# Softmax sums of a fourth attention layer split between GpSimd and VectorE, and a bias moved from GpSimd to ScalarE

## What is computed

```python
qt = conv1x1(x, w_q, b_q).reshape(BS * N_HEADS, H * W, -1)
xp = avg_pool_3x3_s2_same(x)
kt = conv1x1(xp, w_k, b_k).reshape(BS * N_HEADS, H * W // 4, -1)
vt = conv1x1(xp, w_v, b_v).reshape(BS * N_HEADS, H * W // 4, -1)
attn = jnp.einsum('bnd,bmd->bnm', qt, kt) / TEMP
attn = jax.nn.softmax(attn, axis=-1)
out = jnp.einsum('bnm,bmd->bnd', attn, vt)
out = conv1x1(out.reshape(BS, H, W, -1), w_o, b_o)
return out + x
```

## Time and profile before

| what | us |
|---|---|
| median of 3 runs | 139.18 |
| lowest, highest | 138.91, 140.83 |
| the profiled execution | 138.04 |
| its span, first to last instruction | 136.2 |
| busy in it: PE, DVE, ACT, POOL | 121.5, 91.3, 76.1, 59.7 |

### The profile page before, as it was taken

The page is one execution under the profiler, slowest core; times in us unless marked ns, Lnnn a source line. Parts: engine busy times, 40 slices in busy tenths (PEclk is TensorE's granted clock), DMA queues, the critical chain, the costliest instruction groups (busy, mean ns, idle before and its releaser), DMA issues.

```text
span 136.2 us, 3586 instructions
## 1 busy us (share of the span) xinstructions
PE 121.5 (89%) x1391; PEld 90.1 (66%) x1391; DVE 91.3 (67%) x212; ACT 76.1 (56%) x226; POOL 59.7 (44%) x88
## 2 busy tenths in 40 slices
PE   6785999999999999999989993958959999989990
PEld 4464999997776677767668892413315676878990
DVE  5776696999532554588978622669699999950072
ACT  0435445599956548558796752143516476597420
POOL 8941992000000131321038888702365666889400
PEclk9999999999999999999999999999999999999998
DMA  3950000000000000000000024445463500000046
GB/s 94 329 162 0 0 5 2 0 2 0 0 0 5 0 5 0 0 5 0 0 0 0 25 78 112 90 128 82 135 99 116 82 0 5 5 0 5 5 118 190
DMA packets 19104, 6.41 MB, mean 47 GB/s; under 512 B 9360, under 2 KB 18960, under 8 KB 19088
## 3 DMA queue, kind: packets, MB, share of 16 engines
q1 hardware_dynamic: 17456, 4.92, 15.2%
q10 hardware_dynamic: 1632, 1.27, 3.2%
HBM read 4.61 MB, written 1.57 MB: 45 GB/s over the span
## 4 chain that ended last, share of the span: by engine, by line
PE 54%; DVE 32%; DMA 4%; issue 3%; ACT 3%; POOL 1%; ACTq 0%; DVEq 0%
PE bank L677 11%; DVE prob L520 8%; PE bank L622 8%; DVE negmax L518 7%; DVE inv L527 5%; PE bank L720 4%; DMA x_all<-in_x_dram 4%; DVE prob L491 4%; PE bank L661 3%; PE bank L674 3%; PE bank L615 3%; PE bank L737 3%; DVE negmax L482 3%; PE bank L607 3%; PE bank L608 3%
## 5 line engine op out<-in xcount | busy, mean ns | idle before, releaser
L360 ACT ACTIVATE prob<-bank,negmax 128x256 f32<-128x256 f32 (+1 forms) x48 | 19.4, 414 | 16.8 <-DVE negmax L482 16.6
L300 POOL TENSOR_TENSOR prob<-prob,inv 128x512 f32<-128x512 f32 x16 | 16.3, 1042 | 15.5 <-DVE inv L530 15.5
L408 ACT ACTIVATE prob<-prob 128x512 f32<-128x512 f32 x16 | 10.1, 631 | 19.3 <-DVE prob L520 19.3
L699 PE MATMUL bank<-kdiag,qT 128*32 128x512 f32 x128 | 15.4, 597 | 5.9 <-issue 5.9
L291 POOL TENSOR_TENSOR probT<-turned,packed 128x256 f32<-128x256 f32 x8 | 4.9, 612 | 35.5 <-DVE turned L502 35.5
L677 PE MATMUL bank<-probT,v 128*128 128x256 f32 x64 | 16.9, 387 | 0.4 <-issue 0.4
L508 DVE SCALAR_TENSOR_TENSOR xT<-bank,packed,xT 128x256 f32<-128x256 f32 x16 | 7.6, 483 | 13.0 <-PE bank L677 8.3
L622 PE MATMUL bank<-packed,xT 128*128 128x128 f32 x96 | 15.6, 287 | 0.2 <-ACT prob L360 0.2
L622 PEld LDWEIGHTS bank<-packed,xT 128*128 128x128 f32 x96 | 13.2, 191 | 2.1 <-issue 1.2
L677 PEld LDWEIGHTS bank<-probT,v 128*128 128x128 f32 x64 | 11.1, 190 | 3.1 <-issue 2.2
L720 PEld LDWEIGHTS bank<-probT,vdiag 128*32 128x32 f32 x512 | 11.4, 112 | 2.6 <-issue 2.6
(11 more groups left out here) (90 smaller groups left out, 233.4 us busy)
## 6 DMA issues: line engine op xcount, KB each, us to landing
kdiag<-k_rows SPq DMA_DIRECT2D x32, 64.0 KB, 2.4
out_dram<-x_all SPq DMA_DIRECT2D x8, 128.0 KB, 2.0
x_all<-in_x_dram SPq DMA_DIRECT2D x2, 256.0 KB, 4.1
x_all<-in_x_dram ACTq DMA_DIRECT2D x2, 256.0 KB, 5.5
vdiag<-v_rows SPq DMA_DIRECT2D x8, 64.0 KB, 2.9
packed<-in_pack_dram ACTq DMA_DIRECT2D x1, 321.0 KB, 5.8
k_rows<-kT SPq DMA_DIRECT2D x4, 64.0 KB, 2.3
v_rows<-vt SPq DMA_DIRECT2D x4, 64.0 KB, 1.9
```

The costliest lines, as they stand in the source:

```text
L300: nc.gpsimd.tensor_tensor(p, p, inv[g][:, t, :].unsqueeze(2).broadcast_to([128, HEADS, KEYS]), ALU.mult)\
L360: last = nc.scalar.activation(prob[g][:, t, 0:keys], psum("scores", layer, g)[:, keys * t:keys * t + keys], ACT.Exp, bias=negmax[g][:, t, ...
L699: last = mm(ps[STRIP * s:STRIP * s + STRIP, :].rearrange("p (c m k) -> p c k m", c=HEADS, m=HKEY), qT[g][:, 0, HTOK * j:HTOK * j + HTOK], ...
```

## The change

POOL gets a new function, `half_sums(g)`: behind the exponentials of image g it adds the first 32 to the last 32 of each group of 64, in one instruction with 512 outputs for both tiles, and puts them into the first half of `probT[g]`, which is free then. It is issued ahead of the first multiply for image 0, and behind the multiplies of image g for image g+1. DVE's reduction waits for the half sums and reads these 512 columns instead of the 1024 exponentials. The bias of the output goes from POOL, where it was one tensor_scalar an image, to ACT as an Identity activation, at the same place of the list; POOL's wait for the scores ahead of it goes away.

```diff
--- before.py
+++ after.py
@@ -203,6 +203,7 @@
         s_windows, s_turn = sem("windows_spread"), sem("window_step")
         s_max, s_inv, s_scaled = (sem(n) for n in ("max_ready", "inv_ready", "prob_scaled"))
         s_pool, s_xb = sem("pool_step"), sem("output_bias_added")
+        s_sum3 = sem("half_sums3_ready")
         s_key_rows = sem("key_channels_ready")
         s_keys_out, s_vals_out = ([sem(f"{n}_in_dram{i}") for i in range(IMAGES // PAIR)] for n in ("keys", "values"))
         s_keys, s_vals = ([sem(f"{n}_placed{i}") for i in range(IMAGES // PAIR)] for n in ("keys", "values"))
@@ -265,6 +266,12 @@
 
         @block.gpsimd
         def _(pool):
+            def half_sums(g):
+
+                pool.wait_ge(s_exp3, TILES * (g + 1))
+                p = prob[g][:, :, :].rearrange("p t (c x m) -> p (t c) x m", c=HEADS, x=2)
+                nc.gpsimd.tensor_tensor(view(probT[g][:, 0, :], TILES * HEADS), p[:, :, 0, :], p[:, :, 1, :], ALU.add).then_inc(s_sum3, 1)
+
             nc.gpsimd.memset(neg_half[:, :], -0.5).then_inc(s_half, 1)
             pool.wait_ge(s_half, 1)
             for n in range(EARLY, QUARTERS - LATE):
@@ -294,15 +301,15 @@
                         .then_inc(s_windows, 1)
                 if step == "share3":
 
+                    if g == 0:
+                        half_sums(g)
                     pool.wait_ge(s_inv3, 2 * (g + 1))
                     for t in range(TILES):
                         p = view(prob[g][:, t, :], HEADS)
                         nc.gpsimd.tensor_tensor(p, p, inv[g][:, t, :].unsqueeze(2).broadcast_to([128, HEADS, KEYS]), ALU.mult)\
                             .then_inc(s_share3, 1)
-                if step == "xb":
-
-                    wait_filled(pool, "scores1", 3, g)
-                    nc.gpsimd.tensor_scalar(xb[g], xT[g][:, :], part["bo3"], None, ALU.add).then_inc(s_xb, 1)
+                    if g + 1 < IMAGES:
+                        half_sums(g + 1)
                 if step == "pool":
 
                     wait_drained(pool, "o", 2, g)
@@ -411,6 +418,8 @@
                         wait_filled(act, f"probT{t}", 3, g)
                         nc.scalar.activation(probT[g][:, t, :], psum(f"probT{t}", 3, g)[:, :], ACT.Copy)\
                             .then_inc(*drained_by(f"probT{t}", 3, g))
+                if step == "xb":
+                    nc.scalar.activation(xb[g], xT[g][:, :], ACT.Identity, bias=part["bo3"]).then_inc(s_xb, 1)
                 if step == "x":
                     wait_filled(act, "x", 3, g)
                     nc.scalar.activation(y[g], view(psum("x", 3, g)[:, 0:TOK], TILES), ACT.Copy).then_inc(*drained_by("x", 3, g))
@@ -523,8 +532,8 @@
 
             def sums3(g):
 
-                dve.wait_ge(s_exp3, TILES * (g + 1))
-                nc.vector.tensor_reduce(out=inv[g][:, :, :], in_=prob[g][:, :, :].rearrange("p t (c m) -> p t c m", c=HEADS),
+                dve.wait_ge(s_sum3, g + 1)
+                nc.vector.tensor_reduce(out=inv[g][:, :, :].rearrange("p t c -> p (t c)"), in_=view(probT[g][:, 0, :], TILES * HEADS),
                                         op=ALU.add, axis=AX.X).then_inc(s_inv3, 1)
                 dve.wait_ge(s_inv3, 2 * g + 1)
                 nc.vector.reciprocal(inv[g][:, :, :], inv[g][:, :, :]).then_inc(s_inv3, 1)
```

## The result

The changed kernel takes 141.26 us, the median of 16 runs (140.18 to 142.03), against 139.28 us for the kernel before, 16 runs too. The ratio is 1.0157, with a 95% interval of 1.0135 to 1.0178: 1.6% slower, 2.2 us. The forecast was 139.8 us, 0.65 us more than before. The direction and the place are right; the forecast size is a third of what came.

What follows compares the result with a forecast made beforehand. DVE and PE were taken to bound the stage side by side; the POOL-DVE ring, six turns of 4.11 us, ends the last image 0.65 us later. 139.18 + 0.65 = 139.8 us, range 138.4 to 141.4.

Steps and rivals of the forecast that it cites:

- The ring: POOL and DVE: multiplies, half sums, sums, reciprocal wait on each other in a loop; 4.11 us a turn against 4.01 before.
- the half sum: POOL: one addition with 512 outputs per image, taken as 1.04 us from the multiply L300; bounds 1.00 and 1.85.
- What bounds the kernel: Fourth layer's stretch: DVE, turning in 4.01 us, and PE run side by side, so PE's gaps limit any gain.
- The ceiling of about 0.8 us: PE: taking work from DVE can gain no more than PE's own gaps, 0.31 + 0.35 us, and 0.1 at 124.20.
- DVE's sums: DVE's reduction of 512 instead of 1024 columns: 0.63 us in place of 1.16, bounds 0.58 and 0.70.
- the prediction's own signs: Signs of being wrong: DVE turns of 3.5 us, half sums over 1.2 us, or PE waiting for ACT's bias.
- The skill's rule: POOL's half sum: 2.6 cycles an element at 1.2 GHz, estimated 1.11 us; set aside for L300's 1042 ns.
- the first two sums: DVE, images 0 and 1: half sums arrive in time, so these sums really get shorter, 0.53 us each.
- ACT's bias: ACT: eight added Identity activations, at most 470 ns each, hidden by waits; cost 0.
- The bias left on POOL: POOL: had L305 stayed there, a turn would be 4.11 + 0.92 = 5.0 us.
- PE at the end: PE wins 0.4 to 0.6 us near 120, then waits for POOL at image 7's transposes; 0.65 us reaches the end.
- The half sum is dear: Rival, POOL between multiply and DVE's sums: each 0.1 us costs 0.6 at the end; over 2% from 1.4 us; chance 0.1.

Runs made afterwards that it cites:

- run without half sums: Changed kernel without half sums, DVE summing only 512 of the 1024 exponentials: 0.992 (0.9856 to 0.9984) to the kernel before; median of all twelve runs 139.80 us.
- broadcast variant: Changed kernel with the POOL addition's second operand replaced by the group's negated maximum, broadcast: one run, 140.21 us.
- kernel before with earlier keys: Kernel before with SP issuing a pair's value-placing DMAs behind the next pair's key store: 0.9963 (0.9932 to 0.9994).
- kernel with half sums first: Changed kernel with the half sums of image g+1 ahead of POOL's wait for the reciprocal of g and its multiplies: 1.0022 (0.9975 to 1.0069) to the kernel before.

## Why the prediction was right and wrong

The ring was foreseen, and one term of it was mis-sized: the half sum, 1.04 us in place of 1.28. It makes 1.4 of the 1.56 us by which the forecast at the end of the ring was too small.

- *What bounds the kernel.* Right that DVE and PE run side by side: the 4.2 us taken from DVE didn't come through in the run without half sums. The ceiling of about 0.8 us is not shown. It was read from one execution, at 138.04 us faster than any of the 16 runs beside the result; the kernel with only the bias moved stood idle for 1.43 us at a place where that execution has no gap. What I passed over is how near the keys are: PE starts image 4 at 100.29 some 2 us behind SP's last issue, and I used that only to say that DVE doesn't set it. Once DVE turned in 3.48, this was the wait that held the kernel.
- *DVE's sums.* The reduction took 684 ns on average and 0.70 in the chain, my upper bound, where I chose 0.63: behind a wait it costs what L518 costs behind a wait. 6 x 0.07 = 0.4 us.
- *The half sum.* This is the term that failed: 1.04 us forecast, 1.28 measured, at a pitch of 1.25 against 1.02. Six turns of 0.23 are 1.4 us. Half sums of over 1.2 us were one of the prediction's own signs that it is wrong. I took the multiply's duration because it has the same output count, and held L312 against the objection that the multiply streams only one operand. L312 has 128 columns; the line was drawn through it and L300, so it could not tell the two kinds of operand apart. Nor was the upper bound the dearest rate of the trace: L314 took 572 ns for 112 columns, 5.1 ns a column, against L305's 3.6. The broadcast variant shows the cause: 1047 ns with one operand streamed, 1276 with two.
- *The skill's rule.* The Trainium skill ("GPSIMD Engine Reference", "Performance versus the Vector engine") gives 2.6 cycles an element for two inputs at 1.2 GHz, since both come through one read port. I turned that into an estimated 1.11 us and let L300's row overrule it. But L300 streams only one operand, and by the broadcast variant that is the cheaper case. The 1.11 held the elements alone. Rows with a broadcast operand carry 0.18 us besides (612 ns at 256 columns, 1042 at 512); with it the estimate would have been 1.29 us, and the trace has 1.28. That the fixed part is the same for two streamed operands is not shown, so the match to 0.01 us may be luck.
- *The ring.* Right in every link and in its order. Forecast 4.11 us, measured 4.37: +0.23 half sum, +0.07 sums, -0.04 for the handover from POOL to DVE (0.03, not 0.07). Six turns of 0.26 are 1.56, and 0.65 + 1.56 = 2.2 us is what was measured. That the first two sums are each 0.53 us shorter came out nearly: the ring began 0.1 us later than that. DVE's idle time was 0.80 in place of 0.6.
- *ACT's bias.* Right, cost 0: 0.9999 alone. It takes 516 ns, and 0.40 us in a stream.
- *The bias left on POOL.* Wrong: 4.37, not 5.0 or more a turn. I added its time to the ring without looking where in the turn it stands.
- *PE at the end.* The place was right: PE waits for both tiles of image 7, and the ring's delay goes to the end in full. The way there wasn't. Nothing was won at 120: with turns of 4.37 the last exponential began at 119.33, not at the forecast 117.6 (118.29 in the kernel before), and PE came to the transposes at 125.8 in place of 123.7. The two gaps are gone, but PE began the scores of image 4 0.9 us later (101.18 against 100.29), and the slow stretch took another 1.6.
- *The rivals.* "The half sum is dear" had its price right (0.6 us for each 0.1) and its objection right (both operands streamed). Its 0.24 us were in neither case of mine: the forecast ended at a turn of 4.21, and the rival spoke of 1.4 us and more.

## What to carry to other kernels

When a sum is split over two engines, draw the ring before counting load: who waits for whom, and what stands in each queue ahead of the producer. An instruction that could run early must stand ahead of the wait, not behind the work of the step before; that alone was worth 1.3% here. Before a ceiling is read off the gaps of one execution, look at those of a second. For a new operation take the duration of one that streams the same operands, not only one with the same output count. And when a change frees an engine and the time stays, look at the next wait of the bound engine: two DMAs in the wrong place of SP's queue hid 2% here.

## What the runs showed of the hardware

GpSimd's multiplication and addition of 128x512 float32 with one operand broadcast took 1.04 to 1.05 us. Its addition with both operands read at full length took 1.28 us, with contiguous operands and with runs of 32 columns alike.

TensorE's granted clock fell in some executions after PE's waits for keys. In the changed kernel's profile, PE had waited 2.14 us ahead of 101.18:

```profile
101.20:104.20 3.00, 3.00 (x17) 0.67 (x18) 2.13 (x5) 1.60 (x3) 1.91 (x3) 0.62 0.46 100
```

In this row of the view of stretches the seventh value behind the times of its ends is the granted clock, 0.62 on average, so a good part of the stretch ran at 1.2 and not at 2.4 GHz, and the scores took 2.98 us in place of 1.92. In the kernel before with earlier keys, PE waited 2.46 us ahead of its first scores and the clock stayed at 1.00. So the wait alone doesn't decide it, and what does is left open. It doesn't delay DVE in the changed kernel, where the scores are there when DVE comes to them. In the kernel with half sums first, where the slow stretch (3.09 us at 93.98) lies on the chain, it may be a part of why 0.994 wasn't reached; that wasn't measured.
